# Attention with a second pair of tiles for the queries' halves, and a scale row made after attention instead of before it

## The chip, the cores and the metric

The kernel runs on one core of one Trainium2 chip. The metric is the device time of one execution, in microseconds. Each time is the median of several executions.

## What is computed

Two layers over x of 4 x 2048 tokens, each 512 wide, with a context of 4 x 128 keys. Layer 0 is a softmax cross-attention with 16 heads and a feed-forward network whose activations and weights are quantised. Layer 1 is an attention without softmax and a feed-forward stage with tanh.

```python
x = x + _L0_xattn_ref(_layernorm(x), ctx_1024, ctx_1024, Wq, bq, Wk, bk, Wv, bv, Wo, bo, temperature)
x = x + _L0_ffn_ref(_layernorm(x), w1, b1, w2, b2)
x = x + _L1_xattn_ref(_layernorm(x), ctx_1024, ctx_1024, mask, 0, wq_w, wq_b, ..., ln_g, ln_b)
x = x + _L1_ffn_ref(_layernorm(x), weight, aux_weight1, aux_weight2, bias)
```

In the quantised network each row of w2 has a scale, the largest magnitude of the row over 127. One scale for all activations comes from the largest value of the whole layer's input, so it is known only after the last token has passed attention:

```python
def quant_weight_int8_perchannel(w):
    s = jax.lax.stop_gradient(jnp.maximum(jnp.max(jnp.abs(w), axis=1, keepdims=True), EPS)) / 127.0
```

## The kernel before

The program is three blocks, each written as one list of instructions per engine, in an order fixed by hand. At the end of a block all five engines meet at a barrier, and no instruction of the next block starts before it.

**Block 1, `prepare` (0 to 161 us).** It projects the context to keys and values, folds weight matrices together, quantises w1 and w2, and stores intermediates to HBM. The table `kinds` lists its products on TensorE in order; product number p uses PSUM bank p % 6. Its last entries are four products `m`, four transposes `x` of the first token group, the product `row`, and `q`, the projection of queries 0. After `q` comes the projection of queries 1 into the bank `qx`, which attention reads.

The product `row` spreads the scales of w2 over all partitions. VectorE multiplies the identity by each of four scale columns `sw2` (tile `dg`, L595), TensorE multiplies a tile of ones by each (L296), and VectorE copies the bank to `sw2row` (L601). The inputs are float32. TensorE runs each such 128x128 product as two instructions in the trace. `sw2row` is first read in block 3, by VectorE at L1921.

**Block 2, `attend` (161 to 897 us).** One step handles one tile of 512 tokens by 4 heads; there are 64 steps. `queries` projects the tokens (TensorE, bank `x_bank`), `qhi` writes its rounded half to `qT[0]` (ScalarE, L1080), `qlo` writes the remainder to `qT[1]` (VectorE, L1167), and `paired` on the SP queue sends both by 8 DMAs to the planes `qs[o % 2]` that `scores` reads. `qT` is one pair of tiles, `bqreph` and `bqrepl` in the trace, so `qhi` of tile o waits until the DMAs of tile o - 1 have landed (`e_qs`).

`values` multiplies the transposed probabilities by the values into two banks. `vlow` (ScalarE, L1090) copies half of each bank to the tile `vl`, `vsum` (VectorE, L1179) writes bank plus `vl` to the tile `cs`, `chi` (ScalarE, L1098) writes the rounded half of `cs`, and `clo` (GpSimd, L1323) the remainder. `clo` is the last reader of `cs`, so `vsum` of the next tile waits for it.

**Block 3, `rest` (from 897 us).** VectorE reduces the largest input over all tokens in four short instructions (L1889 to L1892). TensorE transposes the result (`turn_top`, L1579), VectorE goes on with five more short instructions, and ScalarE normalises the first group of tokens (`relu(0)`, L1657). Then come the transposes and the first products of the feed-forward network (L1561). In `products`, pair i of group u uses `pairs[i % 3]` of the PSUM tiles. GpSimd's first own instruction is at L1966, after `relu(0)`.

Of the kernel before, what the change touches and what calls it, by code (L numbers as in the profile page):

```python
# [9 lines left out]
ALU = mybir.AluOpType  # L10
# [4 lines left out]
P = 128  # L15
# [68 lines left out]
def cut(i):  # L84
    return slice(i * P, i * P + P)


def prepare(nc, A, scr, ident, identb):
    with ExitStack() as ctx:
        def sb(name, shape, dt=F32):  # L90
            return ctx.enter_context(nc.sbuf_tensor("p_" + name, shape, dt))

        def ev(name, unit=1):
            return Event(scr["sem"]("p_" + name), unit)
# [14 lines left out]
        dg = sb("dg", [P, KC, P])  # L109
# [8 lines left out]
        ones = sb("ones", [P, P])  # L118
# [38 lines left out]
        kinds += ["t1"] * KC + ["m"] * 3 + ["x"] * KC + ["m", "row", "q"]  # L157
        place = {}
        for p, kind in enumerate(kinds):
# [8 lines left out]
        e_zero, e_ident, e_identb, e_ones, e_half, e_diag, e_zeroed = (  # L168
            ev(n) for n in ("zero", "ident", "identb", "ones", "half", "diag", "zeroed"))
# [10 lines left out]
        e_bn, e_mv, e_var, e_rstd, e_dg = ev("bn"), ev("mv"), ev("var"), ev("rstd"), ev("diagonal")  # L180
# [21 lines left out]
        def _(e):  # L202
# [88 lines left out]
            p = place["row"][0]  # L291
            e_ones.wait_ge(e, 0)
            e_dg.wait_ge(e, 0)
            free(p)
            for c in range(KC):
                last = e.matmul(bank[p % 6][:, cut(c)], ones[:], dg[:, c, :], start=True, stop=True)  # L296
            last.then_inc(*e_prod)
# [129 lines left out]
        def _(e):  # L427
# [165 lines left out]
            e_ident.wait_ge(e, 0)  # L593
            for c in range(KC):
                last = e.tensor_scalar(dg[:, c, :], ident[:], scr["sw2"][:, c:c + 1], None, ALU.mult)  # L595
            last.then_inc(*e_dg)
            scr["e_x"][1].wait_ge(e, 0)
            stats(1)
            p = place["row"][0]
            e_prod.wait_ge(e, p)  # L600
            e.tensor_copy(scr["sw2row"][:], bank[p % 6][:]).then_inc(*e_gone)  # L601
# [7 lines left out]
        def _(e):  # L609
# [6 lines left out]
            e.memset(ones[:], 1.0).then_inc(*e_ones)  # L616
# [192 lines left out]
def attend(nc, A, scr, ident):  # L809


    with ExitStack() as ctx:
# [20 lines left out]
        cs, vl = sb("cs", [P, 512]), sb("vl", [P, 512])  # L833
        xb = scr["xb"]
        xT = [scr["v1"], [scr["ctx"][1], sb("xT1l", [P, KC, 512], F32R)]]
        qT = [x[:].rearrange("p c n -> p (c n)") for x in scr["bqrep"]]
# [65 lines left out]
        def half_tile(b, o):  # L902

            return b * (TPB // 2) + o // 2
# [136 lines left out]
        def _(e):  # L1041
# [29 lines left out]
            def qhi(b, kk):  # L1071
                o = kk + QUERY
                if not there(b, o):
                    return
                u, c = b * TPB + o, o % 4
                if isinstance(u, int) and u < ASKED:
                    return
                e_q.wait_ge(e, u - ASKED)
                e_qs[(o - 1) % 2].wait_ge(e, half_tile(b, o - 1))
                e.activation(qT[0], x_bank[:], ACT.Identity, bias=bq[:, c:c + 1]).then_inc(*e_qhi)  # L1080

            def vlow(b, kk):
# [44 lines left out]
        def _(e):  # L1127
# [31 lines left out]
            def qlo(b, kk):  # L1159
                o = kk + QUERY  # L1160
                if not there(b, o):
                    return
                c = o % 4
                if first(b) and o < ASKED:
                    return
                e_qhi.wait_ge(e, b * TPB + o - ASKED)
                e.scalar_tensor_tensor(out=qT[1], in0=x_bank[:], scalar=bq[:, c:c + 1],  # L1167
                                                  in1=f32(qT[0]), op0=ALU.add, op1=ALU.subtract).then_inc(*e_qlo)
# [189 lines left out]
        def _(e):  # L1358
# [53 lines left out]
            def paired(b, kk):  # L1412

                o = kk + QUERY
                if not there(b, o) or first(b) and o < ASKED:
                    return

                if not first(b) or kk >= 0:
                    e_s.wait_ge(e, 4 * (b * TPB + kk) + 3)
                for h, e_half in ((0, e_qhi), (1, e_qlo)):  # L1420
                    e_half.wait_ge(e, b * TPB + o - ASKED)
                    for plane, to, at, n in QUERY_BLOCKS[h]:
                        e.dma_start(f32(qs[o % 2][plane][to:to + n, :]), f32(qT[h])[at:at + n, :])\
                            .then_inc(e_qs[o % 2].sem, 16)
# [23 lines left out]
def rest(nc, A, scr, ident, identb, out):  # L1448
# [3 lines left out]
    with ExitStack() as ctx:  # L1452
# [39 lines left out]
        x3T = [sb(f"x3T{h}", [P, KC, P], F32R) for h in "hl"]  # L1492
        mask, flag, eps = two("mask", [P, TPG, KEYS], U8), two("flag", [P, TPG]), two("eps", [P, TPG])
# [7 lines left out]
        e_xn0 = ev("xn0")  # L1501
        e_relu0 = ev("relu0")
# [50 lines left out]
        def _(e):  # L1553
            def products(u, i):
                if i == 0:
                    e_xT.wait_ge(e, 2 * u + 1)
                e_mx.wait_ge(e, PAIRS * u + i - 3)
                for q in range(2):
                    f = 2 * i + q
                    for k in range(KC):  # L1560
                        last = e.matmul(h_bank[(PAIRS * u + i) % 3][:, q, :], w1[:, k, f * P:f * P + P], xT[u % 2][:, k, :],  # L1561
                                        start=k == 0, stop=k == KC - 1)
                last.then_inc(*e_h)
# [16 lines left out]

            turn_top(e_top, pairs[2], e_all)
# [67 lines left out]
        def _(e):  # L1649
# [67 lines left out]

            e_scale.wait_ge(e, 0)
# [34 lines left out]
        def _(e):  # L1753
# [139 lines left out]
            e_all.wait_ge(e, 0)  # L1893
# [19 lines left out]
            for u in range(NG):  # L1913
                for i in range(PAIRS):
                    hidden(u, i)
                    if i == 3:
                        quantise(u + 2)
                if u in (1, 2, 3, 4):

                    e_b2.wait_ge(e, 0)  # L1920
                    after(e.reciprocal(scr["s2"][:, cut(u - 1)], scr["sw2row"][:, cut(u - 1)]))  # L1921
# [42 lines left out]
        def _(e):  # L1964
            e_xn0.wait_ge(e, TPG - 1)
            e.memset(half[:], -0.5).then_inc(*e_half)  # L1966
            e_half.wait_ge(e, 0)
# [153 lines left out]
def program(nc, A, out):  # L2121
# [3 lines left out]
    with ExitStack() as ctx:  # L2125
# [12 lines left out]
        scr["sw1"], scr["sw2"], scr["sw2row"] = sb("sw1", [P, FC]), sb("sw2", [P, KC]), sb("sw2row", [P, D])  # L2138
# [32 lines left out]
        scr["s2"] = sb("s2", [P, D])  # L2171
# [34 lines left out]
```

## Time and profile before

| quantity | value |
|---|---|
| median of 3 runs | 1807.15 us |
| lowest and highest | 1807.06 and 1807.82 us |
| the profiled execution's own time | 1805.24 us |
| span of that profile | 1803.4 us |
| TensorE busy | 1739.2 us, 96% of the span |
| VectorE busy | 1564.4 us, 87% |
| ScalarE busy | 1203.7 us, 67% |
| GpSimd busy | 970.8 us, 54% |

The profile shows one execution. Its instructions carry the line numbers of the kernel before. The busy shares are means over three blocks with different limits, so what an edit is worth is read at its own place.

### The profile page before, as it was taken

The numbers are of one execution on the slowest core, as the hardware profiler recorded it, in microseconds if no ns is written. First come the engines' busy times: TensorE is split into PE (matmuls) and PEld (weight loads), VectorE is DVE, ScalarE is ACT, GpSimd is POOL, SyncE is SP. The second block draws the span as 40 slices with busy tenths as digits, with TensorE's granted clock in tenths as the row PEclk, the third lists the DMA queues.
The fourth block names the chain that finished last, engine by engine and source line by source line (L and its number), as shares of the span: only waits on it lengthen the run. The fifth ranks groups of instructions, "written<-read, shape, count | busy, mean of one in ns | idle before, by whom it ended". The sixth has DMA issues, their size and how long they took to land.

```text
span 1803.4 us, 29914 instructions
## 1 busy us (share of the span) xinstructions
PE 1739.2 (96%) x9162; PEld 1297.6 (72%) x9162; DVE 1564.4 (87%) x3587; ACT 1203.7 (67%) x3374; POOL 970.8 (54%) x1076
## 2 busy tenths in 40 slices
PE   8998799999999999999799999899999999999997
PEld 7776688888888888888544444467767677776765
DVE  6867799999999999988689888879888988988885
ACT  4675899999999999999443332366555655655543
POOL 2434466666666666666500000257666776766665
PEclk9999999999999999999999999999999999999999
DMA  8766444555465556544389997254455445445311
GB/s 309 222 219 166 113 129 139 157 156 145 142 160 154 145 148 158 148 124 126 103 302 396 403 392 311 83 195 167 153 178 175 167 164 178 170 151 177 119 59 41
DMA packets 153902, 322.08 MB, mean 179 GB/s; under 512 B 47376, under 2 KB 55568, under 8 KB 136080
## 3 DMA queue, kind: packets, MB, share of 16 engines
q1 hardware_dynamic: 153280, 319.38, 54.8%
q8 instruction: 75, 1.23, 0.3%
q10 hardware_dynamic: 464, 0.79, 0.1%
q14 instruction: 83, 0.68, 0.1%
HBM read 163.86 MB, written 105.91 MB: 150 GB/s over the span
## 4 chain that ended last, share of the span: by engine, by line
PE 46%; DVE 1%; issue 1%; ACT 1%; POOL 1%; POOLq 0%; DVEq 0%; ACTq 0%
PE f_pair L1561 12%; PE f_pair L1614 12%; PE f_pair L68 6%; PE f_pair L70 6%; PE f_pair L69 6%; PE f_pair L1601 3%; PE f_pair L1572 1%; ACT f_hf L1682 0%; DVE f_st L1819 0%; POOL f_rs L1978 0%; ACT f_room L1657 0%; POOL f_ring L2006 0%; DVE f_pair L1832 0%; DVE f_x2Tl L1807 0%; POOL f_off L1984 0%
## 5 line engine op out<-in xcount | busy, mean ns | idle before, releaser
L1306 POOL TENSOR_TENSOR a_pr<-a_pr,a_rcp 128x512 f32<-128x512 f32 x256 | 266.4, 1041 | 247.3 <-DVE a_rcp L1148 247.3
L1056 ACT ACTIVATE a_pr<-a_s,a_nmax 128x128 f32<-128x128 f32 x1024 | 343.4, 405 | 28.1 <-DVE a_nmax L1141 25.7
L1561 PE MATMUL f_pair<-f_room,w 128*128 128x512 bf16 x1024 | 228.2, 382 | 0.9 <-ACT f_room L1670 0.9
L1056 ACT ACTIVATION_READ_ACCUMULATOR a_pr<-a_s,a_nmax 128x1 f32 x1024 | 219.7, 215 | 0.0
L1978 POOL TENSOR_TENSOR f_rs<-f_rs,f_half 128x1 f32<-128x1 f32 x128 | 121.2, 947 | 179.9 <-DVE f_rs L1825 179.9
L1779 DVE CUSTOM_DVE_ANT_0 f_hf<-f_pair,nb,sh 128x512 f32<-128x512 f32 x244 | 172.6, 748 | 29.3 <-PE f_pair L1561 27.6
L1561 PEld LDWEIGHTS f_pair<-f_room,w 128*128 128x128 bf16 x1024 | 99.3, 98 | 116.4 <-issue 2.7
L1141 DVE TENSOR_REDUCE a_nmax<-a_s 128x4 f32<-128x512 f32 x256 | 171.9, 671 | 7.3 <-PE a_s L947 7.2
L1156 DVE TENSOR_TENSOR a_pTl<-a_pt,a_pTh 128x512 fp32r<-128x512 f32 x256 | 168.3, 678 | 7.5 <-ACT a_pTh L1068 3.6
L959 PE MATMUL a_pt<-ident,a_pr 128*128 128x128 f32 x1024 | 157.2, 276 | 7.8 <-POOL a_pr L1306 6.0
L1068 ACT ACTIVATE a_pTh<-a_pt 128x512 fp32r<-128x512 f32 x256 | 152.1, 638 | 4.8 <-PE a_pt L959 4.6
L959 PEld LDWEIGHTS a_pt<-ident,a_pr 128*128 128x128 f32 x1024 | 118.0, 140 | 20.6 <-POOL a_pr L1306 10.2
L1614 PE MATMUL f_pair<-w 128*128 128x512 bf16 x512 | 118.2, 385 | 2.1 <-DVE w L1787 2.1
L1971 POOL MEMSET f_room<- 128x1 f32 x2 | 0.1, 98 | 221.0 <-PE f_pair L1572 221.0
L1614 PE MATMUL f_pair<-w,f_room 128*128 128x512 bf16 x512 | 117.8, 384 | 0.0
L1682 ACT ACTIVATE f_hf<-f_hf,f_col 128x2048 f32<-128x2048 f32 x57 | 113.8, 1997 | 0.0
L68 PE MATMUL f_pair<-wch,f_x3Th 128*128 128x512 f32 x256 | 101.3, 396 | 3.1 <-DVE f_x3Tl L1807 3.1
L1009 PE MATMUL a_v<-a_pTh,a_vp 128*128 128x512 f32 x256 | 100.9, 394 | 1.7 <-DVE a_pTl L1156 1.4
L1009 PE MATMUL a_v<-a_pTl,a_vp 128*128 128x512 f32 x256 | 100.6, 393 | 0.0
L70 PE MATMUL f_pair<-wch,f_x3Tl 128*128 128x512 f32 x256 | 100.6, 393 | 0.0
L69 PE MATMUL f_pair<-wcl,f_x3Th 128*128 128x512 f32 x256 | 100.0, 391 | 0.0
L1708 ACT ACTIVATE f_room<-xr,f_off,f_rs 128x512 f32<-128x512 f32 (+1 forms) x64 | 52.1, 815 | 69.1 <-POOL f_off L1984 69.1
(442 smaller groups left out, 5068.4 us busy)
## 6 DMA issues: line engine op xcount, KB each, us to landing
hidden<-f_hf SPq DMA_DIRECT2D x57, 1024.0 KB, 9.0
f_hf<-hidden SPq DMA_DIRECT2D x57, 1024.0 KB, 4.8
xr<-x SPq DMA_DIRECT2D x96, 256.0 KB, 3.2
xb<-x SPq DMA_DIRECT2D x16, 1024.0 KB, 5.4
x<-xr SPq DMA_DIRECT2D x64, 256.0 KB, 2.3
ctxh<-bqreph SPq DMA_DIRECT2D x126, 128.0 KB, 2.4
f_room<-x SPq DMA_DIRECT2D x15, 1024.0 KB, 10.8
ctxh<-bqreph SPq DMA_DIRECT2D x128, 64.0 KB, 2.1
```

The lines of the kernel that those rows point to most:

```text
L68: e.matmul(out, ah, bh, start=first, stop=False)
L69: e.matmul(out, ah, bl, start=False, stop=False)
L70: return e.matmul(out, al, bh, start=False, stop=last)
L959: last = e.transpose(pt_bank[t % 2][:, j * P:j * P + P], pr[:, t, j, :], ident[:])
L1009: last = e.matmul(v_bank[j // 2][:], vp[c][:, j, :], pT[h][:, j, :], start=j % 2 == 0 and h == 0, stop=j % 2 == 1 and h == 1)
L1056: last = e.activation(pr[:, t, j, :], s_bank[t][:, j * P:j * P + P], ACT.Exp, bias=nmax[kk % 2][:, t, j:j + 1], accum_out=sums[t][:, j:j + 1])
L1141: e.tensor_reduce(nmax[kk % 2][:, t, :], s_bank[t][:].rearrange("p (j n) -> p j n", j=4), AX, ALU.max, negate=True).then_inc(*e_max)
L1156: e.tensor_tensor(pT[1][:, :, at], pt_bank[t % 2][:].rearrange("p (j n) -> p j n", j=4), f32(pT[0][:, :, at]), ALU.subtract).then_inc(*e_plo)
L1306: e.tensor_tensor(p, p, rcp[kk % 2][:, t, :].unsqueeze(2).to_broadcast([P, 4, KEYS]), ALU.mult).then_inc(*e_pn)
L1561: last = e.matmul(h_bank[(PAIRS * u + i) % 3][:, q, :], w1[:, k, f * P:f * P + P], xT[u % 2][:, k, :], start=k == 0, stop=k == KC - 1)
L1614: last = e.matmul(y_bank[w % 2], hq[g % 2][:, f, cut(t)], w2[:, f, :], start=f == 0, stop=f == FC - 1)
L1779: last = e.tensor_tensor_reduce(out=hbuf(n)[:, f % 4, :], in0=h_bank[(PAIRS * u + i) % 3][:, q, :], in1=scr["nb1"][:, f:f + 1].to_broadcas ...
```

## The change

It has three parts. First, `qT` becomes two pairs of tiles, and tile o uses pair o % 2; `qhi` of tile o waits for the DMAs of tile o - 2. Second, the tile `vl` goes: `vlow` copies straight into `cs`, `vsum` adds the bank in place, and the wait for `clo` of the tile before moves from `vsum` on VectorE to `vlow` on ScalarE. Third, the product `row` leaves block 1. Block 3 makes it: GpSimd writes the tile of ones and the four columns of `dg`, TensorE multiplies them ahead of `turn_top`, and ScalarE copies the bank to `sw2row` ahead of `relu(0)`.

```diff
-        kinds += ["t1"] * KC + ["m"] * 3 + ["x"] * KC + ["m", "row", "q"]
+        kinds += ["t1"] * KC + ["m"] * 3 + ["x"] * KC + ["m", "q"]
...
-            p = place["row"][0]
-            e_ones.wait_ge(e, 0)
-            e_dg.wait_ge(e, 0)
-            free(p)
-            for c in range(KC):
-                last = e.matmul(bank[p % 6][:, cut(c)], ones[:], dg[:, c, :], start=True, stop=True)
-            last.then_inc(*e_prod)
...
-            e_ident.wait_ge(e, 0)
-            for c in range(KC):
-                last = e.tensor_scalar(dg[:, c, :], ident[:], scr["sw2"][:, c:c + 1], None, ALU.mult)
-            last.then_inc(*e_dg)
             scr["e_x"][1].wait_ge(e, 0)
             stats(1)
-            p = place["row"][0]
-            e_prod.wait_ge(e, p)
-            e.tensor_copy(scr["sw2row"][:], bank[p % 6][:]).then_inc(*e_gone)
...
-        cs, vl = sb("cs", [P, 512]), sb("vl", [P, 512])
+        cs = sb("cs", [P, 512])
...
-        qT = [x[:].rearrange("p c n -> p (c n)") for x in scr["bqrep"]]
+        qT = [[x[:].rearrange("p c n -> p (c n)") for x in scr["bqrep"]], [sb(f"qT1{h}", [P, 512], F32R)[:] for h in "hl"]]
...
                 e_q.wait_ge(e, u - ASKED)
-                e_qs[(o - 1) % 2].wait_ge(e, half_tile(b, o - 1))
-                e.activation(qT[0], x_bank[:], ACT.Identity, bias=bq[:, c:c + 1]).then_inc(*e_qhi)
+                if not first(b) or o >= 2:
+                    e_qs[o % 2].wait_ge(e, half_tile(b, o - 2))
+                e.activation(qT[o % 2][0], x_bank[:], ACT.Identity, bias=bq[:, c:c + 1]).then_inc(*e_qhi)
...
                     e_pv.wait_ge(e, 2 * u + i)
-                    e_vs.wait_ge(e, 2 * (u - 1) + i)
-                    e.activation(vl[64 * i:64 * i + 64, :], v_bank[i][64 - 64 * i:128 - 64 * i, :], ACT.Copy).then_inc(*e_vl)
+                    e_clo.wait_ge(e, u - 1)
+                    e.activation(cs[64 * i:64 * i + 64, :], v_bank[i][64 - 64 * i:128 - 64 * i, :], ACT.Copy).then_inc(*e_vl)
...
-                e_clo.wait_ge(e, u - 1)
                 e_vl.wait_ge(e, 2 * u + i)
                 at = slice(64 * i, 64 * i + 64)
-                e.tensor_tensor(cs[at, :], v_bank[i][at, :], vl[at, :], ALU.add).then_inc(*e_vs)
+                e.tensor_tensor(cs[at, :], v_bank[i][at, :], cs[at, :], ALU.add).then_inc(*e_vs)
...
+        ones, dg = sb("ones", [P, P]), scr["s2"]
...
+                if (u, i) == (0, 1):
+                    e_sw2.wait_ge(e, 0)
...
+            e_half.wait_ge(e, 0)
+            for c in range(KC):
+                last = e.matmul(pairs[1][:, 0, cut(c)], ones[:], dg[:, cut(c)], start=True, stop=True)
+            last.then_inc(*e_all)
             turn_top(e_top, pairs[2], e_all)
...
+            e_all.wait_ge(e, 0)
+            e.activation(scr["sw2row"][:], pairs[1][:, 0, :], ACT.Copy).then_inc(*e_sw2)
             e_scale.wait_ge(e, 0)
             relu(0)
...
-            e_all.wait_ge(e, 0)
+            e_all.wait_ge(e, 1)
...
+            e.memset(ones[:], 1.0)
+            for c in range(KC):
+                last = e.tensor_scalar(dg[:, cut(c)], ident[:], scr["sw2"][:, c:c + 1], None, ALU.mult)
+            last.then_inc(*e_half)
             e_xn0.wait_ge(e, TPG - 1)
```

VectorE at the end of block 1, before the change: `v1l` is the low half of the transposed tokens, `p_st` and `p_mv` are the statistics of the second token group, `bqrepl` is the low half of queries 0.

```order
L509 TENSOR_TENSOR v1l<-p_bank,v1h 128x512 x2
L595 TENSOR_SCALAR p_dg<-ident,sw 128x128 x4
L559 BN_STATS p_st<-xb 128x6 x4
L563 BN_AGGR p_mv<-p_st 128x2 x4
L566 TENSOR_SCALAR p_rs<-p_mv 128x4
L601 COPY sw2row<-p_bank 128x512
L604 SCALAR_TENSOR_TENSOR bqrepl<-p_bank,bq,bqreph 128x512
L572 TENSOR_SCALAR xb<-xb,p_mv,p_rs 128x512 x4
```

The same place on VectorE, with the change:

```order
L500 TENSOR_TENSOR v1l<-p_bank,v1h 128x512 x3
L550 BN_STATS p_st<-xb 128x6 x4
L554 BN_AGGR p_mv<-p_st 128x2 x4
L557 TENSOR_SCALAR p_rs<-p_mv 128x4
L588 SCALAR_TENSOR_TENSOR bqrepl<-p_bank,bq,bqreph 128x512
L563 TENSOR_SCALAR xb<-xb,p_mv,p_rs 128x512 x4
```

The four multiplications for `dg` and the copy to `sw2row` are gone, and nothing else has moved.

TensorE at the start of block 3, before the change: `f_room` holds the reduced column in its first instruction and the tokens in the later ones, `f_pair` is a pair of PSUM banks, `w` is w1.

```order
L812 UNCONDITIONAL_BRANCH
L1552 UNCONDITIONAL_BRANCH
L1579 MATMUL f_pair<-ident,f_room 128x128
L1585 MATMUL f_pair<-identb,f_room 128x128 x16
L1561 MATMUL f_pair<-f_room,w 128x512 x32
```

The same place on TensorE, with the change; `s` is the room of `s2`, which holds `dg`:

```order
L795 UNCONDITIONAL_BRANCH
L1537 UNCONDITIONAL_BRANCH
L1570 MATMUL f_pair<-s,f_ones 128x128 x4
L1566 MATMUL f_pair<-ident,f_room 128x128
L1576 MATMUL f_pair<-identb,f_room 128x128 x16
L1548 MATMUL f_pair<-f_room,w 128x512 x32
```

Four float32 products now stand ahead of the transpose for which VectorE waits, and they wait in turn for GpSimd's first five instructions of the block.

## Rows read from the trace of the kernel before

**Rows 1.** The head of the profile's page.

```profile
span 1803.4 us, 29914 instructions
```

**Rows 2.** Windows: length; PE, PEld, DVE, ACT, POOL busy (count); clock, DMA share, GB/s.

```profile
400.00:550.00 150.00, 149.80 (x866) 129.77 (x866) 144.37 (x366) 138.09 (x559) 100.33 (x102) 1.00 0.55 148
905.50:1140.00 234.50, 234.50 (x1255) 113.16 (x1256) 201.72 (x533) 76.54 (x94) 0.13 (x2) 0.99 0.90 349
```

**Rows 3.** The line L1080 (`qhi`): ScalarE's idle time before it.

```profile
  DMA ctxh<-bqrepl: 8.4, 6
```

**Rows 4.** Timeline of one steady step of attention: `clo`, then the next tile's `vlow`.

```profile
499.37 1.29 POOL L1323 TENSOR_TENSOR a_cT1l<-a_cs,a_cT1h 128x512 fp32r<-128x512 f32 x1
505.10 0.59 ACT L1090 ACTIVATE a_vl<-a_v 64x512 f32<-64x512 f32 x1
```

**Rows 5.** Timeline of block 1's end: start, duration, engine, line, instruction, idle time before.

```profile
151.06 1.28 DVE L509 TENSOR_TENSOR v1l<-p_bank,v1h 128x512 fp32r<-128x512 f32 x2
152.26 0.86 DVE L595 TENSOR_SCALAR p_dg<-ident,sw 128x128 f32<-128x128 f32 x4
153.22 1.13 PE L296 MATMUL p_bank<-p_dg,p_ones 128*128 128x128 f32 x8 [0.90 <-issue]
154.11 0.48 PE L68 MATMUL p_bank<-v1h,wqh 128*128 128x512 f32 x1
154.69 0.53 SPq L723 DMA_DIRECT2D w_quantised<-p_wst  x1
156.03 0.68 DVE L601 COPY sw2row<-p_bank 128x512 f32<-128x512 f32 x1
159.37 1.26 SPq L196 DMA_DIRECT2D ctxh<-bqrepl  x2
```

**Rows 6.** DMA issues at 154 to 155.5 us: size, time from issue to landing.

```profile
w_quantised<-p_wst SPq DMA_DIRECT2D x1, 512.0 KB, 5.4
```

**Rows 7.** Timeline of attention's start.

```profile
161.35 1.29 DVE L1231 BATCH_NORM_STATS2 a_st<-xb 128x6 f32<-128x512 f32 x2 [0.89 <-PEq L89]
161.93 0.10 POOL L1296 MEMSET a_half<- 128x4 f32 x1 [4.69 <-POOLq L89]
163.20 0.69 ACT L1080 ACTIVATE bqreph<-qx,bq 128x512 fp32r<-128x512 f32 x1 [5.34 <-DMA ctxh<-bqrepl]
164.23 0.15 DVE L1236 BATCH_NORM_AGGREGATE a_mv<-a_st 128x2 f32<-128x6 f32 x1
164.29 0.72 DVE L1167 SCALAR_TENSOR_TENSOR bqrepl<-qx,bq,bqreph 128x512 fp32r<-128x512 f32 x1
```

**Rows 8.** Timeline of block 3's start, up to the first products of the network.

```profile
897.86 0.23 DVE L1889 TENSOR_TENSOR f_mx<-mx,mean 128x64 f32<-128x64 f32 x1 [0.36 <-PEq L812]
898.92 0.33 PE L1579 MATMUL f_pair<-ident,f_room 128*128 128x128 f32 x1 [4.20 <-DVE f_room L1892]
899.28 0.29 DVE L1894 TENSOR_REDUCE f_col<-f_pair 128x1 f32<-128x128 f32 x1 [0.42 <-PE f_pair L1579]
900.55 2.93 ACT L1657 ACTIVATE f_room<-xr,qb,qa 128x512 f32<-128x512 f32 x4 [18.71 <-DVE qb L1898]
905.50 1.04 PE L1561 MATMUL f_pair<-f_room,w 128*128 128x512 bf16 x2 [0.90 <-ACT f_room L1670]
```

**Rows 9.** Groups of GpSimd's 128x128 work, by form: count, busy us, mean ns, idle before.

```profile
L662 POOL TENSOR_TENSOR xr<-xr,ident 128x128 f32<-128x128 f32 x12 | 8.2, 687 | 0.0
L615 POOL CAST identb<-ident 128x128 bf16<-128x128 f32 x1 | 0.3, 289 | 0.1
L616 POOL MEMSET p_ones<- 128x128 f32 x1 | 0.2, 204 | 0.0
```

**Rows 10.** Windows of half a microsecond in which the granted clock changed.

```profile
169.00:169.50 0.50, 0.50 (x4) 0.40 (x3) 0.00 (x0) 0.50 (x4) 0.46 (x1) 0.81 0.35 111
899.50:900.00 0.50, 0.00 (x0) 0.00 (x0) 0.40 (x4) 0.00 (x0) 0.00 (x0) 0.64 0.65 78
909.50:910.00 0.50, 0.50 (x3) 0.15 (x1) 0.50 (x2) 0.00 (x0) 0.00 (x0) 0.62 0.06 20
```

More of the change, by code:

```diff
@@ L108, in prepare @@
         cols = sb("cols", [P, 4, KC])
-        dg = sb("dg", [P, KC, P])
         rows = sb("rows", [P, 3, D])
@@ L117, in prepare @@
         means, whole = sb("means", [P, KC + 1]), sb("whole", [P, 1])
-        ones = sb("ones", [P, P])
         st, mv = sb("st", [P, 2, TPG, 6]), sb("mv", [P, 2, TPG, 2])
@@ L167, in prepare @@
         e_small, e_rows, e_row3 = ev("small", 16), ev("rows", 16), ev("row3", 16)
-        e_zero, e_ident, e_identb, e_ones, e_half, e_diag, e_zeroed = (
-            ev(n) for n in ("zero", "ident", "identb", "ones", "half", "diag", "zeroed"))
+        e_zero, e_ident, e_identb, e_half, e_diag, e_zeroed = (
+            ev(n) for n in ("zero", "ident", "identb", "half", "diag", "zeroed"))
         e_chi, e_clo, e_whi, e_wlo = ev("chunkhi"), ev("chunklo"), ev("weighthi"), ev("weightlo")
@@ L179, in prepare @@
         e_wst, e_mout = [ev(f"w2out{i}", 16) for i in range(2)], [ev(f"mout{i}", 16) for i in range(4)]
-        e_bn, e_mv, e_var, e_rstd, e_dg = ev("bn"), ev("mv"), ev("var"), ev("rstd"), ev("diagonal")
+        e_bn, e_mv, e_var, e_rstd = ev("bn"), ev("mv"), ev("var"), ev("rstd")
         e_centred, e_folded, e_bias, e_base, e_eye = ev("centred"), ev("folded"), ev("biasrow"), ev("baserow"), ev("eye")
@@ L615, in _ @@
             e.tensor_copy(identb[:], ident[:]).then_inc(*e_identb)
-            e.memset(ones[:], 1.0).then_inc(*e_ones)
             e.memset(half[:], -0.5).then_inc(*e_half)
@@ L1166, in qlo @@
                 e_qhi.wait_ge(e, b * TPB + o - ASKED)
-                e.scalar_tensor_tensor(out=qT[1], in0=x_bank[:], scalar=bq[:, c:c + 1],
-                                                  in1=f32(qT[0]), op0=ALU.add, op1=ALU.subtract).then_inc(*e_qlo)
+                e.scalar_tensor_tensor(out=qT[o % 2][1], in0=x_bank[:], scalar=bq[:, c:c + 1],
+                                                  in1=f32(qT[o % 2][0]), op0=ALU.add, op1=ALU.subtract).then_inc(*e_qlo)
             def vsum(b, kk, i):
@@ L1422, in paired @@
                     for plane, to, at, n in QUERY_BLOCKS[h]:
-                        e.dma_start(f32(qs[o % 2][plane][to:to + n, :]), f32(qT[h])[at:at + n, :])\
+                        e.dma_start(f32(qs[o % 2][plane][to:to + n, :]), f32(qT[o % 2][h])[at:at + n, :])\
                             .then_inc(e_qs[o % 2].sem, 16)
@@ L1501, in rest @@
         e_xn0 = ev("xn0")
+        e_sw2 = ev("scalerowkept")
         e_relu0 = ev("relu0")
@@ L1920, in _ @@
                     e_b2.wait_ge(e, 0)
+                    e_sw2.wait_ge(e, 0)
                     after(e.reciprocal(scr["s2"][:, cut(u - 1)], scr["sw2row"][:, cut(u - 1)]))
@@ L1964, in _ @@
         def _(e):
+            e.memset(ones[:], 1.0)
+            for c in range(KC):
+                last = e.tensor_scalar(dg[:, cut(c)], ident[:], scr["sw2"][:, c:c + 1], None, ALU.mult)
+            last.then_inc(*e_half)
             e_xn0.wait_ge(e, TPG - 1)
             e.memset(half[:], -0.5).then_inc(*e_half)
-            e_half.wait_ge(e, 0)
+            e_half.wait_ge(e, 1)
             e_w.wait_ge(e, 10)
@@ L2136, in program @@
         }
-        scr["sw1"], scr["sw2"], scr["sw2row"] = sb("sw1", [P, FC]), sb("sw2", [P, KC]), sb("sw2row", [P, D])
+        scr["sw1"], scr["sw2"] = sb("sw1", [P, FC]), sb("sw2", [P, KC])
         scr["mean1"], scr["rstd1"], scr["mx1"] = (sb(n, [P, NT]) for n in ("mean1", "rstd1", "mx1"))
@@ L2170, in program @@
         scr["wch"] = [sb(f"wc{h}", [P, KC, D], F32R) for h in "hl"]
-        scr["s2"] = sb("s2", [P, D])
+        scr["s2"], scr["sw2row"] = sb("s2", [P, D]), sb("sw2row", [P, D])
         scr["rows"] = sb("rows", [P, 3, D])
```

## The prediction

> **What bounds the kernel now.** I read four views, in this order. The page's head gives the span, 1803.4 us [rows 1]. The windows then say where TensorE leaves time free. In 150 us of steady attention it is busy for 149.80 us, and in the first pass of the network for 234.50 of 234.50 us [rows 2]. In both stretches TensorE's own work sets the time, so taking a wait from another engine can gain nothing there. The idle time of line L1080 shows what the second pair of tiles is about. ScalarE waited 8.4 us in all for the DMAs out of `qT`, before 6 of its instructions, and 5.34 us of that stand before a single one, at attention's start [rows 3, 7]. Last come the timelines of the two seams between blocks, where TensorE stands still and short chains decide [rows 5, 7, 8]. The change touches both seams, so I price it there.
>
> **The second pair of tiles.** In the steady part ScalarE's waits sum to 8.4 - 5.3 = 3.1 us in 5 pieces, under work with which TensorE is full. I take 0. If that cover were gone, the price would be the 3.1 us.
>
> At attention's start the wait ends at 163.20 us, but the next reader isn't free any earlier. VectorE starts its statistics right after the barrier at 161.35 us and is busy with them until 164.38 us, while `qhi` has been done since 163.20 + 0.69 = 163.89 us. The low half starts at 164.29 us, right behind the statistics' last instruction [rows 7]. An earlier `qhi` therefore starts nothing earlier on VectorE. Of the 5.34 us, most is the wait for the barrier. I take 0 here too. The bound on the gain is what ScalarE waited past VectorE's start, 163.20 - 161.35 = 1.85 us.
>
> **Values summed in place.** The two copies and the two sums keep their number and size. The wait for `clo` now stands on ScalarE, and behind it are the next exponentials. In a steady step `clo` ends at 499.37 + 1.29 = 500.66 us, and the next `vlow` starts at 505.10 us [rows 4]. That leaves 4.4 us of slack, so the wait is over before it is asked for. I take 0. It would cost from the point at which `clo` came 4.4 us late; then each of 64 steps would lose the excess.
>
> **The row leaves block 1.** VectorE loses four multiplications, 0.86 us, and a copy, 0.68 us. TensorE loses 0.90 us of waiting and the eight instructions of the product; from 153.22 to 154.11 us they take 0.89 us. The query product could then start when the low halves of the transposed tokens are done, at 151.06 + 1.28 = 152.34 us in place of 154.11 us. That is 1.77 us earlier, and everything behind it (the halves of queries 0 on ScalarE and VectorE, the DMAs of them on SP) moves with it [rows 5].
>
> The barrier won't follow all the way. SP waits at the end of the block for the stores of the quantised w2. The last of them is issued at 154.69 us [rows 5], behind work that doesn't move, and lands 5.4 us later, at 160.09 us [rows 6]. Today SP's last issue ends at 159.37 + 1.26 = 160.63 us, after that landing, and the queries' DMAs set the barrier. With the change this issue would end at 158.86 us, so the store is late next. The gain is 160.63 - 160.09 = 0.54 us. Its bounds are 0, if the store lands later among the earlier query DMAs, and 1.77 us, if it was done sooner than the row says. I take -0.5 us.
>
> **The row enters block 3.** Here a chain of short instructions sets the end. VectorE makes the column, TensorE transposes it at 898.92 us, VectorE goes on at 899.28 us, `relu(0)` starts at 900.55 us, and the first products start at 905.50 us [rows 8]. Behind them TensorE is full for the rest of the pass [rows 2], so what is lost here isn't recovered. The transpose now has five instructions of GpSimd and four products ahead of it.
>
> - GpSimd's start: at the other seam its first instruction came 161.93 - 161.35 = 0.58 us after VectorE's [rows 7]. From 897.86 us [rows 8] that gives 898.44 us.
> - The tile of ones: 0.20 us, from the same instruction in block 1 [rows 9].
> - Four multiplications of 128x128 by a column: no row on GpSimd. The bounds are 0.29 us each, a cast with one input, and 0.69 us each, an addition with two inputs, some of it beside VectorE's work [rows 9]. Since only one input is a full tile, I go near the cast and take 0.35 us each, 1.4 us together. GpSimd is done at 900.04 us.
> - Four float32 products: 0.89 us at the full clock [rows 5]. In the trace the granted clock fell to half (1.2 GHz) in the window that starts at 899.50 us [rows 10], after TensorE had stood idle for 4.20 us before the transpose [rows 8]. At half clock they take 1.78 us, until 901.82 us.
> - The transpose and the step to VectorE: 899.28 - 898.92 = 0.36 us [rows 8], some 0.45 us at half clock. VectorE goes on at 902.3 us.
>
> The delay is 902.3 - 899.28 = 3.0 us. With the lower bounds (GpSimd starts with VectorE, 0.29 us each, full clock) it is 897.86 + 0.20 + 1.16 + 0.89 + 0.36 - 899.28 = 1.2 us. With the upper ones it is 898.44 + 0.20 + 2.75 + 1.78 + 0.45 - 899.28 = 4.3 us. ScalarE's copy of the row, about 0.7 us as other full tiles of ScalarE [rows 7], hides behind the 1.27 us that VectorE needs from the transpose to `relu(0)` [rows 8].
>
> The Trainium skill, GPSIMD Engine Reference, section Engine selection, says that work with one input runs on GpSimd about as fast as on VectorE, and work with two inputs about half as fast. VectorE's four took 0.86 us, so by that rule the delay would be some 0.5 us shorter. The case's two rows, 0.29 and 0.69 us, lie apart in the same sense.
>
> **The clock behind it.** Before, the dense products started at 905.50 us and the full clock (2.4 GHz) came back within the window from 909.50 us, after some 4.2 us [rows 8, 10]. At the other seam it took from 163.2 to some 169.2 us, 6 us. Products at half clock lose half of such a stretch, 2.1 and 3 us. With the change the clock may return between at once and 6 us after the start, so this term lies between -2.1 and +0.9 us. I take 0.
>
> The Trainium skill, TensorE: Matmul & The Clock Gate, section What's actually happening, says that the gate's watch runs free of the kernel, so the same code meets it at another phase from run to run. The two stretches of 4.2 and 6 us fit that. If it holds, the sign of this term isn't settled by one trace.
>
> **The sum.** 0 + 0 - 0.5 + 3.0 + 0 = +2.5 us. The profiled execution took 1805.24 us, 1.9 us under the median of 1807.15 us; its span is 1803.4 us. The profile gives 1807.7 us, the median 1809.6 us.
>
> **The rivals.**
>
> - Faster (chance 0.07): the wait for `qT` is on the path after all. The mechanism is the 5.34 us at attention's start, of which 1.85 us lie after the barrier, with 3.1 us in the steady part and the full 1.77 us of block 1. Together they give -6.7 + 3.0 = -3.7 us, 1803.4 us. It turns the sign once more than 3.0 us of it reach TensorE. For it speaks that ScalarE is the engine with the longest single stall there. Against it speaks that TensorE is full in the windows.
> - Nothing lost at the second seam (0.20): GpSimd is early, the products run at full clock, and the clock returns sooner. 1.2 - 1.5 - 0.5 = -0.8 us, 1806.3 us. For it speaks that the window of the clock's fall starts only 0.5 us before the products.
> - A dearer second seam (0.20): GpSimd's multiplications at 0.69 us, since its first ones run beside VectorE's additions of two inputs, and a late clock. 4.3 + 0.9 - 0.5 = +4.7 us, 1811.9 us. The Trainium skill, GPSIMD Engine Reference, section Key points, says that GpSimd shares its way to SBUF with VectorE and that VectorE instructions with two SBUF inputs contend. It would make this one likelier in the first 0.5 us of the block; VectorE's idle time then ends that.
> - The moved wait for `clo` stalls ScalarE (0.03): +0.2 us per step would be 64 x 0.2 = 12.8 us. The slack of 4.4 us speaks against it.
>
> **How the numbers follow.** My forecast has 0.50. A measurement of this kernel can tell a change from none at about 0.2%, which is 3.6 us. Slower by more needs nearly the upper bound at the seam, so I give all of the dear rival but a little, and the stall: 0.20 in all. Faster by more needs nearly all of the first rival: 0.06. The rest, 0.74, lies within. For the range I leave out the first rival and the stall; it goes from 1806.0, below the cheap seam, to 1812.2, above the dear one.
>
> **What the profile of the changed kernel would show.** VectorE's first instruction of attention stands at about 160.8 us, and SP's last wait of block 1 is for the w2 store. `qhi` has no idle time for a DMA, while the steady windows stay at 149.8 of 150 us on TensorE. At block 3 the transpose comes some 3 us later behind VectorE's first instruction than the present 1.06 us, and the first products start some 10.6 us behind it, now 7.64 us. I am wrong if attention itself gets shorter or longer by over 1 us, if the barrier follows the queries by the full 1.77 us, or if GpSimd is done before VectorE's column.

## The result, and the profile after

The changed kernel takes 1808.65 us, the median of 20 runs (1807.17 to 1811.24). The kernel before took 1807.11 us beside it (20 runs, 1804.68 to 1808.49). The ratio is 1.0013, with a 95% interval of 1.0007 to 1.0019, and the means differ by 2.4 ± 0.8 us (two standard errors, as in all such differences below). The forecast was 1809.6 us and no change by the bound of 0.2%.

The head of the page of the changed kernel answers to [rows 1]. The span is 3.1 us longer.

```profile
span 1806.5 us, 29790 instructions
```

The windows of the changed kernel answer to [rows 2]; the second one covers nearly all of steady attention. TensorE now has no idle time in it. The same stretch of 590 us held 589.37 us of TensorE's work before, so 0.63 us of gaps are gone. Attention as a whole, from VectorE's first instruction in it to its first in block 3, took 736.43 us, before 736.51 us; the half clock cost 7.8 us in it and 6.2 us before (summed as in the table below).

```profile
400.00:550.00 150.00, 150.00 (x869) 130.02 (x868) 144.75 (x368) 138.74 (x561) 100.91 (x102) 1.00 0.54 148
260.00:850.00 590.00, 590.00 (x3412) 511.31 (x3411) 561.92 (x1406) 545.21 (x2192) 396.29 (x398) 1.00 0.53 146
```

The timeline of the end of block 1 and the start of attention answers to [rows 5, 7].

```profile
152.51 0.47 PE L68 MATMUL p_bank<-v1h,wqh 128*128 128x512 f32 x1
154.79 0.53 SPq L706 DMA_DIRECT2D w_quantised<-p_wst  x1
158.79 1.27 SPq L194 DMA_DIRECT2D ctxh<-bqrepl  x2
161.28 1.29 DVE L1214 BATCH_NORM_STATS2 a_st<-xb 128x6 f32<-128x512 f32 x2 [2.44 <-PEq L89]
161.69 0.69 ACT L1064 ACTIVATE a_qT1h<-qx,bq 128x512 fp32r<-128x512 f32 x1 [5.46 <-remote]
164.22 0.72 DVE L1151 SCALAR_TENSOR_TENSOR a_qT1l<-qx,bq,a_qT1h 128x512 fp32r<-128x512 f32 x1
```

The query product starts 1.60 us earlier, at 152.51 us, yet SP's last issue moves by only 0.58 us and the barrier by 0.07 us. The DMA issues of 154 to 155.5 us (size, us to landing) answer to [rows 6].

```profile
w_quantised<-p_wst SPq DMA_DIRECT2D x1, 512.0 KB, 5.9
```

The view of waits on SP at the block's end (who waits, for whom: us, times, longest):

```profile
SPq L55 <- DMA w_quantised<-p_wst: 0.5, 1, 0.5
```

SP does end the block in the wait for this store, which lands at 154.79 + 5.9 = 160.7 us. In attention `qhi` waits for no DMA of `qT` any more, while the low half stays where it was, at 164.22 us behind the statistics.

The timeline of block 3's start answers to [rows 8].

```profile
897.67 0.20 POOL L1959 MEMSET f_ones<- 128x128 f32 x1 [0.85 <-POOLq L795]
897.71 0.23 DVE L1882 TENSOR_TENSOR f_mx<-mx,mean 128x64 f32<-128x64 f32 x1 [0.61 <-PEq L795]
897.86 2.38 POOL L1961 TENSOR_SCALAR s<-ident,sw 128x128 f32<-128x128 f32 x4
900.29 2.07 PE L1570 MATMUL f_pair<-s,f_ones 128*128 128x128 f32 x8 [5.98 <-POOL s L1961]
902.16 0.42 PE L1566 MATMUL f_pair<-ident,f_room 128*128 128x128 f32 x1
902.62 0.29 DVE L1887 TENSOR_REDUCE f_col<-f_pair 128x1 f32<-128x128 f32 x1 [3.71 <-PE f_pair L1566]
903.88 2.93 ACT L1648 ACTIVATE f_room<-xr,qb,qa 128x512 f32<-128x512 f32 x4 [0.88 <-DVE qb L1891]
908.83 1.04 PE L1548 MATMUL f_pair<-f_room,w 128*128 128x512 bf16 x2 [0.90 <-ACT f_room L1661]
```

The chain is as forecast: GpSimd, then the product at half clock, then the transpose, for which VectorE waits 3.71 us. From VectorE's first instruction to `relu(0)` it is 903.88 - 897.71 = 6.17 us, before 2.69 us, so the seam costs 3.48 us. The first products start 11.12 us behind VectorE's first instruction, before 7.64 us, which is again 3.48 us more. From them to the end of the span it is 897.67 us, before 897.90 us.

### The profile page after: what moved, and what is told of

Its sections match the earlier page's. It is cut to its first block, busy times and chain, and to the rows that moved or that the text cites. A ratio compares the mean times of both kernels' runs of the same rounds, so it can differ in the third digit from the quotient of the medians.

```text
span 1806.5 us, 29790 instructions
## 1 busy us (share of the span) xinstructions
PE 1740.2 (96%) x9162; PEld 1298.2 (72%) x9162; DVE 1563.3 (87%) x3582; ACT 1204.6 (67%) x3375; POOL 973.5 (54%) x1080
## 4 chain that ended last, share of the span: by engine, by line
PE 46%; DVE 1%; issue 1%; ACT 1%; POOL 1%; POOLq 0%; DVEq 0%
PE f_pair L1548 12%; PE f_pair L1605 12%; PE f_pair L68 6%; PE f_pair L70 6%; PE f_pair L69 6%; PE f_pair L1592 3%; PE f_pair L1559 1%; ACT f_hf L1673 0%; DVE f_st L1812 0%; POOL f_rs L1976 0%; ACT f_room L1648 0%; POOL f_ring L2004 0%; DVE f_pair L1825 0%; DVE f_x2Tl L1800 0%; POOL f_off L1982 0%
## 5 line engine op out<-in xcount | busy, mean ns | idle before, releaser
L1661 ACT ACTIVATE f_room<-f_pair 128x1024 bf16<-128x1024 bf16 x31 | 31.7, 1024 | 103.6 <-PE f_pair L1559 102.6
```

## The experiments

My theory was that the row's place in block 3 costs some 3.5 us, which the rest hardly pays back. The rivals were that the in-place sum or the single parts of block 1 had a price of their own, and that the second pair of tiles is worth something, so that the seam costs less than it seems. The kernels of one group of four ran on one chip with the kernel before, which then took 1807.17 us (first group), 1806.06 us (second) and 1807.95 us (third), medians of 33 to 35 runs. Kernels of different groups are compared only by their ratios to it.

**The in-place sum alone**, on the kernel before:

```diff
-                    e_vs.wait_ge(e, 2 * (u - 1) + i)
-                    e.activation(vl[...], v_bank[i][...], ACT.Copy).then_inc(*e_vl)
+                    e_clo.wait_ge(e, u - 1)
+                    e.activation(cs[...], v_bank[i][...], ACT.Copy).then_inc(*e_vl)
...
-                e_clo.wait_ge(e, u - 1)
-                e.tensor_tensor(cs[at, :], v_bank[i][at, :], vl[at, :], ALU.add).then_inc(*e_vs)
+                e.tensor_tensor(cs[at, :], v_bank[i][at, :], cs[at, :], ALU.add).then_inc(*e_vs)
```

> The kernel before with one part of the change alone: the tile vl is gone, the copy goes straight into cs and the sum is made in place. Theory 1 (the row's new place at the second seam is the whole loss): no part of attention moves. VectorE's first instruction of block 2 to its first of block 3 takes 736.5 us as before, within 0.3 us, and the time is that of the kernel before within 0.1%. Theory 2 (the wait for clo, now on ScalarE, costs in attention what a faster block 1 or the pairs give back): attention is longer by 1 us or more.

Measured: 1806.66 us, ratio 1.0002 (0.9992 to 1.0013), span 1803.3 us. In its profile the time from `relu(0)` back to VectorE's first instruction, the gaps of steady attention and the time behind the first products all stay within 0.3 us of before. The in-place sum shows neither a cost nor a gain; the means are 0.5 ± 1.8 us apart.

**The row's move alone**, on the kernel before (the third part of the change, with one pair `qT` and with `vl`):

```diff
-        kinds += ["t1"] * KC + ["m"] * 3 + ["x"] * KC + ["m", "row", "q"]
+        kinds += ["t1"] * KC + ["m"] * 3 + ["x"] * KC + ["m", "q"]
...
+            e_half.wait_ge(e, 0)
+            for c in range(KC):
+                last = e.matmul(pairs[1][:, 0, cut(c)], ones[:], dg[:, cut(c)], start=True, stop=True)
             turn_top(e_top, pairs[2], e_all)
```

> The kernel before with the third part alone: the scale row leaves block 1 and is made at the start of block 3. Theory 1: this alone gives the changed kernel's time, 1.5 to 3.5 us over the kernel before (ratio 1.001 to 1.002). From VectorE's first instruction of block 3 to relu(0) it takes 6.2 us as in the changed kernel, against 2.7 us before, and the barrier behind block 1 comes at 161.3 us. Theory 2 (attention's parts take a share): the ratio differs from the changed kernel's by over 0.05%, and attention's length from 736.4 us by over 0.5 us.

Measured: 1809.31 us, ratio 1.0016 (1.0005 to 1.0028), span 1806.6 us, means 2.8 ± 1.7 us apart. `relu(0)` starts 6.18 us behind VectorE's first instruction, as with the whole change. The move alone is enough for the whole loss; whether the other parts give something back, this run can't say within its 1.7 us. Two expected figures were missed: the barrier came at 160.50 us and not at 161.3 us, and attention took 737.5 us and not 736.4 us.

**The change without the second pair:**

```diff
-                if not first(b) or o >= 2:
-                    e_qs[o % 2].wait_ge(e, half_tile(b, o - 2))
-                e.activation(qT[o % 2][0], x_bank[:], ...)
+                e_qs[(o - 1) % 2].wait_ge(e, half_tile(b, o - 1))
+                e.activation(qT[0], x_bank[:], ...)
...
```

`qlo` and `paired` use the one pair in the same way.

> The changed kernel with the second pair of tiles undone: qT is one pair again, and qhi waits for the DMAs of the tile before. Theory 1: ScalarE's idle time for DMAs before qhi comes back, some 8 us in 6 places, and the time stays that of the changed kernel within 0.1%, attention's length 736.4 us within 0.5 us. Theory 2 (the pairs gain, hidden in the sum by a dearer seam): it is slower than the changed kernel by 1 us or more, and attention is longer by as much.

Measured: 1809.61 us, ratio 1.0011 (1.0002 to 1.0020), span 1808.0 us. By this ratio the pair is worth nothing; by the span it is 1.5 us. ScalarE's waits for the DMAs came back (10.4 us before 7 instructions), and attention took 738.64 us in this profile, 2.2 us longer than with the pair. So the traces spoke for the second theory and the times did not. It was taken up again below.

**The row's product behind the transpose**, and ScalarE's copy behind its first copy of tokens:

```diff
-            e_half.wait_ge(e, 0)
-            for c in range(KC):
-                last = e.matmul(pairs[1][:, 0, cut(c)], ones[:], dg[:, cut(c)], start=True, stop=True)
-            last.then_inc(*e_all)
             turn_top(e_top, pairs[2], e_all)
+            e_half.wait_ge(e, 0)
+            for c in range(KC):
+                last = e.matmul(pairs[1][:, 0, cut(c)], ones[:], dg[:, cut(c)], start=True, stop=True)
+            last.then_inc(*e_all)
...
```

> The changed kernel with the row's product behind turn_top on TensorE, and the copy of it behind the first half's copy (copy(0, 0)) on ScalarE. GpSimd's work stays where it is. Theory 1: VectorE gets its transpose some 1.1 us after its first instruction again, and relu(0) starts 2.7 us after it, not 6.2 us. The product then runs while TensorE waits for relu(0), and the time is the kernel before's within 0.1%, some 2 to 3.4 us under the changed kernel's. Rival (GpSimd's work itself slows VectorE's chain, or the product now delays the first transposes): relu(0) or the first products come 0.5 us or more later than in the kernel before, and a part of the loss stays.

Measured: 1804.74 us, ratio 0.9986 (0.9977 to 0.9994), means 2.1 ± 1.0 us under the kernel before, which is more than the 0.1% expected. The timeline of its block 3:

```profile
899.82 0.23 DVE L1882 TENSOR_TENSOR f_mx<-mx,mean 128x64 f32<-128x64 f32 x1 [0.61 <-PEq L795]
900.07 0.33 DVE L1883 TENSOR_TENSOR f_mx<-f_mx,rstd 128x64 f32<-128x64 f32 x1
900.70 0.32 DVE L1885 COPY f_room<-f_col 128x128 f32<-128x128 f32 x1
901.07 0.47 PE L1566 MATMUL f_pair<-ident,f_room 128*128 128x128 f32 x1 [4.65 <-DVE f_room L1885]
902.40 2.07 PE L1571 MATMUL f_pair<-s,f_ones 128*128 128x128 f32 x8 [0.85 <-POOL s L1961]
902.84 2.93 ACT L1648 ACTIVATE f_room<-xr,qb,qa 128x512 f32<-128x512 f32 x4 [19.48 <-DVE qb L1891]
907.80 1.46 PE L1548 MATMUL f_pair<-f_room,w 128*128 128x512 bf16 x3 [0.90 <-ACT f_room L1661]
```

The product of 2.07 us now lies in TensorE's own idle time, and `relu(0)` starts 3.02 us behind VectorE's first instruction, 0.33 us more than before. Some 0.2 us of it are VectorE's: two of its short instructions took 0.33 and 0.32 us beside GpSimd's multiplications, and before, with GpSimd idle, 0.23 us each:

```profile
898.12 0.23 DVE L1890 TENSOR_TENSOR f_mx<-f_mx,rstd 128x64 f32<-128x64 f32 x1
898.63 0.23 DVE L1892 COPY f_room<-f_col 128x128 f32<-128x128 f32 x1
```

The rest is the transpose at half clock, 0.47 us in place of 0.33 us. From the first products to the end it is 896.90 us, which is 1.00 us less than before. Most of that lies in the clock: in windows of a quarter of a microsecond it was back at full 3.0 us after the first products, against 4.5 us in the kernel before and 4.2 us with the change. Half of the 1.5 us less at half clock is 0.75 us.

**The w2 store ahead of the last loads of block 1**, to see what holds the barrier:

```diff
+            send_w2(3)
             load(X2)
             send_m(3, (3,))
-            send_w2(3)
```

> The changed kernel with SP's order at the end of block 1 turned: the last store of the quantised w2 goes out ahead of the load of a token group and of the last store of m. Theory 1 (that store, landing last, holds the barrier and eats what the missing row gives back): SP no longer waits for it after the queries' DMAs, and the barrier comes 0.4 to 1.2 us earlier, at 160.1 to 160.9 us, where now the end of SP's own issues holds it. The time is 0.4 to 1.2 us under the changed kernel's, less than this measurement tells. Rival (the barrier is held by the DMAs' load as a whole): the barrier stays at 161.3 us within 0.2 us.

Measured: 1808.36 us, ratio 1.0011 (1.0003 to 1.0020). This and the next were to show whether the store is all that block 1's gain fails on. The view of waits on SP now names another transfer:

```profile
SPq L55 <- DMA m_all<-xr: 0.7, 1, 0.7
```

**The same store first, with the product behind the transpose** (both edits above):

> Both mends together: the row's product behind turn_top, its copy behind copy(0, 0), and the store of w2 ahead in SP's order. Theory 1: relu(0) 2.7 to 3.1 us after VectorE's first instruction of block 3, the barrier of block 1 at 160.1 to 160.9 us, and a time 2 to 4 us under the kernel before (ratio 0.998 to 0.999). Rival (the run with the product behind was fast by chance, since its blocks add up to the kernel before): a ratio of 1.000.

Measured: 1804.40 us, ratio 0.9986 (0.9977 to 0.9995), the same as without the store's move. The barriers of the two stood at 158.94 and 161.04 us, where 160.1 to 160.9 us had been expected. No half clock fell into block 1 of the first one, and with none there the barrier stood at 159.37 and 159.35 us in two profiles without this edit; the second one lost 1.6 us to it, as most profiles did, and its barrier is no earlier than theirs. The store is not the only thing late: SP's wait moves on to the store of `m_all` in both, and no gain beyond the noise is left.

**The product behind the transpose, one pair of tiles** (the edits of the third and fourth experiment):

> The product behind turn_top, as before, with the second pair of tiles undone. Theory 1 (the pairs give at most the 0.6 us of TensorE's idle time in steady attention): between 250 and 850 us TensorE's idle pieces of 0.2 us are back, and the time is that with the pairs plus 0 to 0.8 us. Rival (the pairs are what makes the version with the product behind faster than the kernel before): the ratio to the kernel before goes from 0.9986 to 1.000.

Measured: 1806.89 us, ratio 1.0004 (0.9995 to 1.0013). On the same chip the version with the pair, which also has the w2 store first, took 1804.40 us, and the means are 2.4 ± 1.2 us apart. The ratio went to 1.000 as the rival had it. The two differ in the store's place as well, but that alone showed nothing at the ratios of 1.0011 and 0.9986 above.

**The tile of ones and the columns made by VectorE**, ahead of its reduction. The lines with a minus stood in GpSimd's list, those with a plus stand in VectorE's:

```diff
-            e.memset(ones[:], 1.0)
-            for c in range(KC):
-                last = e.tensor_scalar(dg[:, cut(c)], ident[:], scr["sw2"][:, c:c + 1], None, ALU.mult)
...
+            e.memset(ones[:], 1.0)
+            for c in range(KC):
+                last = e.tensor_scalar(dg[:, cut(c)], ident[:], scr["sw2"][:, c:c + 1], None, ALU.mult)
             after(e.tensor_tensor(mx[:], scr["mx1"][:], mean[:], ALU.subtract))
```

> The changed kernel with the tile of ones and the four columns made by VectorE, ahead of its own chain, in place of GpSimd. The order on TensorE stays. Theory 1 (of the 3.5 us lost before relu(0), GpSimd's 2.6 us are the larger part and the product's 1.9 us stands behind them): VectorE needs 1.3 us for them, as 0.28 us each in block 1, the product starts 1.4 us after VectorE's first instruction in place of 2.6 us, and relu(0) starts 4.0 to 5.0 us after it, not 6.2 us. The time is 1 to 2 us under the changed kernel's. Rival (the product on TensorE is nearly all of it): relu(0) stays within 0.5 us of 6.2 us.

Measured: 1805.98 us, ratio 1.0003 (0.9994 to 1.0011). Its timeline, to be read against GpSimd's 2.38 us above:

```profile
897.92 0.17 DVE L1882 MEMSET f_ones<- 128x128 f32 x1 [0.67 <-PEq L795]
898.00 0.77 DVE L1884 TENSOR_SCALAR s<-ident,sw 128x128 f32<-128x128 f32 x4
898.83 2.08 PE L1570 MATMUL f_pair<-s,f_ones 128*128 128x128 f32 x8 [4.36 <-DVE s L1884]
902.42 2.93 ACT L1648 ACTIVATE f_room<-xr,qb,qa 128x512 f32<-128x512 f32 x4 [0.88 <-DVE qb L1895]
```

VectorE makes the same four in 0.77 us. `relu(0)` starts 4.50 us after the block's first instruction, 1.67 us sooner than with the change. So 1.7 of the seam's 3.48 us come from having GpSimd and not VectorE make the columns. In time it took 1.8 ± 1.6 us less than the changed kernel with the w2 store first, on the same chip. VectorE's next two instructions of the same kind took 0.23 us again, with GpSimd idle:

```profile
898.94 0.23 DVE L1887 TENSOR_TENSOR f_mx<-f_mx,rstd 128x64 f32<-128x64 f32 x1
899.45 0.23 DVE L1889 COPY f_room<-f_col 128x128 f32<-128x128 f32 x1
```

**The pair once more, on one chip.** The changed kernel and the version with the product behind the transpose, each with two pairs and with one:

> The changed kernel once more, unchanged, as the yardstick for the three others on the same chip. Ratio to the kernel before 1.001 to 1.0025 under every theory.

> The changed kernel with one pair of tiles for the queries' halves. Theory A, the second pair is worth only the 0.6 us of TensorE's gaps in steady attention: within 1.0 us of e3_after. Theory B, it also spares a stretch of half clock at attention's opening, as the two traces without it showed: 1.5 to 3 us slower than e3_after.

> The changed kernel with the row's product behind the transpose, as timed before on another chip: 2.0 to 2.8 us faster than the kernel before, 4 to 4.5 us faster than e3_after.

> The row's product behind the transpose, and one pair of tiles for the queries' halves. Theory A: within 1.0 us of e3_behind. Theory B: 1.5 to 3 us slower than e3_behind, so about as long as the kernel before.

| kernel | median us | ratio (95%) | span | TensorE's gaps in 260 to 850 us | lost to half clock, whole span |
|---|---|---|---|---|---|
| changed kernel | 1808.98 | 1.0012 (1.0003 to 1.0020) | 1805.2 | 0.00 | 17.2 |
| the same, one pair | 1811.09 | 1.0018 (1.0007 to 1.0029) | 1808.7 | 2.14 | 16.7 |
| product behind | 1804.82 | 0.9981 (0.9972 to 0.9989) | 1807.1 | 0.00 | 23.3 |
| the same, one pair | 1806.76 | 0.9997 (0.9989 to 1.0006) | 1807.3 | 1.64 | 20.4 |

The last column is worked out from windows of 2 us: (1 - granted clock) x TensorE's busy time, summed. The product's place (with that of the copy), on one chip, is worth 4.3 ± 1.4 us with two pairs (rows one and three) and 4.2 ± 1.8 us with one (rows two and four), and 4.0 ± 1.4 us in the two kernels with the w2 store first. At the seam it is 3.48 - 0.33 = 3.15 us, and the shorter time behind the first products adds to it. The pair is worth 1.9 ± 1.6 us in the first two rows and 2.0 ± 1.6 us in the last two, in line with 2.4 ± 1.2 us above. The timeline of the changed kernel with one pair shows the mechanism at one of its places:

```profile
382.48 0.69 ACT L1063 ACTIVATE bqreph<-qx,bq 128x512 fp32r<-128x512 f32 x1 [2.23 <-DMA ctxh<-bqrepl]
383.20 0.75 DVE L1150 SCALAR_TENSOR_TENSOR bqrepl<-qx,bq,bqreph 128x512 fp32r<-128x512 f32 x1 [1.40 <-ACT bqreph L1063]
384.01 0.66 PE L917 MATMUL qx<-ident,xb 128*128 128x128 f32 x4 [0.94 <-DVE bqrepl L1150]
...
388.31 0.66 PE L942 MATMUL a_pt<-ident,a_pr 128*128 128x128 f32 x4 [0.23 <-POOL a_pr L1288]
```

The DMA is late, `qhi` waits 2.23 us for it, `qlo` for `qhi`, and TensorE waits 0.94 us because the bank `qx` that `qlo` reads is still taken. A few microseconds later it waits again for probabilities. With two pairs no such row is there.

Both sizes lie in the range of theory B, 1.5 to 3 us, and not in that of theory A. B's mechanism, an extra stretch of half clock near 177 us with one pair, fell all the same. The version with the product behind the transpose and two pairs has it too, in the window below, and the changed kernel with one pair on the same chip had none.

```profile
176.00:178.00 2.00, 2.00 (x6) 1.49 (x7) 1.64 (x5) 1.80 (x10) 0.42 (x1) 0.50 0.51 134
```

In the changed kernel's own profile the same window stood at full clock:

```profile
176.00:178.00 2.00, 1.96 (x11) 1.70 (x12) 1.36 (x3) 1.69 (x8) 1.04 (x1) 1.00 0.47 123
```

Not tried: the pair alone, or the pair with the in-place sum, on the kernel before. All measurements of the pair are on kernels with the row in block 3. The three parts belong together by their room: the second pair takes 2 x 512 x 4 = 4096 bytes per partition, the in-place sum frees the 2048 bytes of `vl`, and the row's move frees the 2048 bytes of `sw2row`, which the changed kernel allocates only after attention.

## Why the prediction was right, and where its terms were off

**The sum held, with terms mis-sized in opposite senses.** Forecast +2.5 us, measured +2.4 ± 0.8 us, and 1.2 ± 1.2 us when the changed kernel ran once more. The mechanism that sets the sign, the row at the head of block 3, was right. That the number was met so closely is luck in part: by the terms below the change comes to 3.5 - 0.4 - 2 - 0.2 = +0.9 us at one end and 3.5 - 0.1 - 1 - 0.2 = +2.2 us at the other.

**The row enters block 3: +3.0 forecast, 3.48 measured.** The order of the chain was right, and so was the half clock: the product took 902.16 - 900.29 = 1.87 us to the transpose, forecast 1.78. Two parts of the term were off. GpSimd began with VectorE (897.67 against 897.71 us), not 0.58 us behind it, so the delay at the other seam didn't carry over. Its multiplications took 2.38 us in all, not 1.4 us. The two errors have opposite signs, which is why the term is off by only 0.5 us. They were priced near the cast because only one input is a full tile, at 0.35 us; their group in the changed kernel says 612 ns:

```profile
L1961 POOL TENSOR_SCALAR s<-ident,sw 128x128 f32<-128x128 f32 x4 | 2.4, 612 | 0.0
```

That is nearer the two-input row of 687 ns [rows 9]. Contention with VectorE explains little of it: the four took 602 to 627 ns, and the last two, with VectorE idle from 898.59 + 0.32 = 898.91 us on, still took 602 ns each. The Trainium skill, GPSIMD Engine Reference, section Engine selection, has work with one input at about VectorE's speed. The runs differ: VectorE took 0.77 us for the same four, a third of GpSimd's time. The choice of the nearest row was the weak step; the upper bound of 4.3 us covered it.

**The row leaves block 1: -0.5 forecast, 0.07 in the profile.** The named cover was right: SP ends the block in the wait for the w2 store. The store landed at 160.7 us and not at 160.09 us, and the bound "0, if the store lands later among the earlier query DMAs" came close to true. The size isn't settled by one profile, because block 1 itself changes length. In seven profiles without the row in block 1 (one of them with the w2 store first) and with a like loss to half clock in it (1.5 to 1.7 us) the barrier stands at 160.87 us on the mean (160.34 to 161.28), and in the two with the row at 161.18 and 161.35 us. That is 0.4 us in favour of the forecast, with a spread of about its own size. Where no half clock fell into block 1 it stood at 158.9 to 159.4 us in three profiles, and with 3.1 us lost at 161.7 and 162.3 us in two.

**The second pair: 0 forecast, about -1 to -2 measured.** This is the step whose reasoning failed. I read 149.80 of 150 us as a TensorE that is full, and took the stalls of ScalarE to be hidden under it. At attention's start that held: the low half stayed behind the statistics. In the steady part the missing 0.20 us was a real gap, and it closed to 150.00 us where the prediction had it stay at 149.8 us. In seven profiles with one pair the 590 us from 260 us on held 0.2 to 2.1 us of such gaps, 0.9 us on the mean. In the seven with two pairs they held at most 0.03 us. The timed pairs of kernels on one chip say 1.9, 2.0 and 2.4 us, each with an error of 1.2 to 1.6 us, while the ratios of 1.0011 and 1.0013 from two chips said nothing. Attention's length says the same, once what the half clock cost in it is taken off (an estimate, summed as in the table but in windows of a quarter of a microsecond). It was 730.5 us on the mean in the seven profiles with one pair (728.2 to 732.6) and 728.5 us in the seven with two (727.8 to 729.2), 1.9 ± 1.2 us less. The gaps are 0.9 us of that. The rest isn't idle time of TensorE elsewhere in attention, 23.7 us with one pair and 23.9 us with two; it lies in time that the traces count as busy, and its cause stays open.

**The in-place sum: 0,** and the run of it alone agrees, within 1.8 us.

**The clock: 0 forecast, -0.2 in the profile** (897.67 against 897.90 us behind the first products), within its bounds.

**The rivals.** "Faster" had its mechanism in part: its steady part is real, but the 1.85 us at attention's start and the 1.77 us of block 1 did not come, so the sign never turned. "Nothing lost at the second seam" fell with `relu(0)`'s 6.17 us. "A dearer second seam" was right on GpSimd's price, though VectorE beside it lengthened the multiplications by 25 ns at most; it was VectorE's own two instructions that took 0.1 us more each. The stall on `clo` didn't appear.

**The better version** keeps all three parts and puts the product behind the transpose. It ran at 0.9986, 0.9986 (with the w2 store first) and 0.9981 of the kernel before. By parts, `relu(0)` costs 0.33 us more than before, the time behind the first products is 1.00 us shorter, and the pair gives 1 to 2 us: 0.33 - 1.00 - 1.5 = -2.2 us, against a measured -2.1 ± 1.0, -1.8 ± 1.0 (with the w2 store first) and -3.1 ± 1.3 us.

## What to carry to other kernels

At a seam where TensorE stands still, the order of a side product against the one on which the chain hangs is worth more than its length: 2.07 us of work cost 3.5 us with its inputs ahead of the transpose, and 0.33 us behind it. "Busy 149.80 of 150" is not full; look for the few gaps, see whether a late buffer makes them, and read more than one execution, for these gaps varied from 0.2 to 2.1 us. When a trace has no row for an instruction on an engine, let the dearer neighbour take part in the central estimate, not only in the bound.

## What the runs showed of the hardware

**The half clock comes at other places from execution to execution.** The window at 102 us in block 1 of the changed kernel was at half clock, and in another profile of the same kernel at full clock:

```profile
102.00:104.00 2.00, 2.00 (x17) 1.91 (x16) 2.00 (x8) 0.71 (x4) 0.18 (x1) 0.50 0.89 323
```

```profile
102.00:104.00 2.00, 2.00 (x23) 1.83 (x23) 2.00 (x7) 0.90 (x5) 0.51 (x2) 1.00 0.71 269
```

Fourteen profiles lost 16.2 to 23.5 us of TensorE's work to it in all. This is a good part of the spread that limits every comparison here. The 35 runs of the kernel before in the third group show it: the two at a mean clock of 0.989 took 1803.9 us on the mean, the twelve at 0.986 took 1808.8 us, the two at 0.984 took 1811.6 us. A change of 1 us can't be seen in one profile's span, only in its segments. The Trainium skill, TensorE: Matmul & The Clock Gate, section What's actually happening, has the gate's watch run free of the kernel, and these rows agree.

**Work right ahead of the first transposes went with an earlier full clock.** In the five profiles in which the row's product lay there, the clock was back 2.3 to 3.0 us after the first products. In the eight in which TensorE stood idle there, it was 3.4 to 4.5 us. One profile speaks against a simple rule: with the columns made by VectorE TensorE's order was that of the change, with the idle time, and the clock was back after 2.9 us. There it had fallen at 896.5 us, 2.3 us before the product, in the six others of that order 0.7 to 1.4 us before it. So the place of the fall counts too, and what decides it stays open. Fourteen single profiles of ten kernels show the link; no run changed this alone.
